# The row of maxima of the second and fourth attention goes through DRAM by DMA in a four-layer cross-attention kernel

## The chip, the cores and the metric

The kernel runs on one core of one Trainium2 chip, as one launch. The metric is the device time of that launch in microseconds. Lower is better.

## The reference, cut to what matters

The model has four layers on 2048 tokens (8 sequences of 256) of width 128. Each layer is a cross attention onto a context of 256 tokens of width 96 per sequence and then a feed-forward part; both are scaled by a tanh gate and added to the residual `x`. The change touches the second and the fourth attention (`L1` and `L3`), which have the same form with other weights:

```
x = x + jnp.tanh(g_xattn[1]) * _L1_xattn_ref(_layernorm(x, axis=-1), ctx_768, Wq, Wk, Wv, Wo, bo)

def _L1_xattn_ref(x, context, Wq, Wk, Wv, Wo, bo):
    q = (x @ Wq).reshape(B, Nq, 16, 64)
    k = (context @ Wk).reshape(B, Nk, 16, 64)
    v = (context @ Wv).reshape(B, Nk, 16, 64)
    scores = jnp.einsum('bqhd,bkhd->bhqk', q, k) / sqrt(64)
    attn = jax.nn.softmax(scores, axis=-1)
    out = jnp.einsum('bhqk,bkhd->bqhd', attn, v).reshape(B, Nq, 1024)
    return out @ Wo + bo
```

Each query attends to the 256 context tokens of its own sequence, in 16 heads. The third attention (`L2`) has 8 heads of 128 and lets each query attend to all 2048 context tokens; the first has 16 heads of 8.

## The kernel before, in words

**Folding.** For each head the product of the query and key weights is formed once (`A`, 128x96), and that of the value and output weights too (`C`, 96x129 with a column that gives the denominator). So a head's queries are `A` times the normalised tokens, in the 96 dimensions of the context, and both scores and values use the context itself. Precision comes from splitting each operand in a high and a low float16 part and adding three products.

**The function.** `attention(nc, M, layer)` (L736) does the second, third and fourth attention. The third is `wide`; the other two, narrow, are those that the change is about. The queries are worked through in blocks of 512 (`NQ` = 4 blocks per head, so 64 blocks in 16 heads). The five engines each run their own stream, with semaphores between them, and the order of the work in a block is written out by hand in three lists at L783 to L785, one for TensorE, one for VectorE, one for ScalarE. In block (h, qb) the streams do work for three heads' worth of stages at once:

- "q": the queries of head h+1, block qb (`queries`, three matmuls L874 to L876 into job bank 0); ScalarE copies them to `q_hi` (L997) and VectorE makes `q_lo` (L1057), which frees bank 0.
- "st": the scores of the next block, keys on partitions (`scores`, 12 matmuls of 256 columns, L913 to L915).
- "m" 0 and 1: rough scores with queries on partitions (`maxscores`, two matmuls of 256 columns each, L894, into job bank 2), of which VectorE takes the negated maxima per query into `nmax` (L1067).
- "r": the row of maxima (`maxrow`, L900). The maxima lie as columns, one query per partition. Four matmuls with one stationary column each and the identity as moving operand (L905) turn them to a row of 512 in bank 0, once that is free; ScalarE copies the row to partition 96 of `q_hi` (L1002), which frees bank 0. The matmul of `scores` with a contraction of 97 then subtracts the maximum as part of the product.
- "exp" on ScalarE (L1009, L1011), "lo" on VectorE (L1097), "av" 0 and 1 on TensorE (the values, 12 matmuls of 256 columns, L925 to L927, into one bank), "u" on ScalarE (copies their result out, L1034).
- "o" 0 and 1: the projection of the previous block's result (`project` of TensorE, L938, four matmul passes of 129 columns into job bank 1). VectorE takes the reciprocal of the denominators ("d", L1081) and adds the two tiles to `x` ("x", L1091), which frees bank 1. "o" 0 and "o" 1 both use bank 1, so "o" 1 waits for "x" 0.

TensorE's order in a block is

```
q, st, m 0, av 0, o 0, r, av 1, m 1, o 1
```

and VectorE's is `q, m 0, d 0, x 0, lo, m 1, d 1, x 1`; ScalarE's is `q, exp, r, u`. The maxima taken in a block are those of the block four further on; the row made in a block is that of the block three further on (`row_of`, `maxrow(blk + NQ - 1, ...)`), and the scores computed in a block are those of the next one.

**The prologue of an attention** does "q", "m 0", "m 1" and "r" for the four blocks of head 0 (no "r" after the last of them), one after the other, since "q" and "r" share bank 0. Then come the first scores. **The last head** prepares no next head: its blocks have no "q" and no "m", and only its first has an "r".

SyncE issues no DMA and GpSimd does nothing but set semaphores while an attention of this function runs.

Of the kernel before, what the change touches and what calls it, by code (L numbers as in the profile page):

```python
# [79 lines left out]
def persistent(nc, ctx):  # L80
    M = Memory()

    def sb(name, shape, dt):
        return ctx.enter_context(nc.sbuf_tensor(name, shape, dt))

    M.x = sb("x_res", [P, NT, D], F32)
    M.xn = sb("x_norm", [P, NT, D], F32)
    M.xt = sb("x_normT", [P, NTOK], F32)
    M.xt_hi = sb("x_normT_hi", [P, NTOK], F16)
    M.xt_lo = sb("x_normT_lo", [P, NTOK], F16)  # L90
    M.ct_hi = sb("ctxT_hi", [DA, NTOK], F16)
    M.ct_lo = sb("ctxT_lo", [DC, NTOK], F16)
    M.cv_hi = sb("ctx_hi", [P, NT, P], F16)
    M.cv_lo = sb("ctx_lo", [P, NT, P], F16)
    M.A_hi = [n and sb(f"A{n}_hi", [P, L.H, DC], F16) for n, L in enumerate(LAYERS)]
    M.A_lo = [n and sb(f"A{n}_lo", [P, L.H, DC], F16) for n, L in enumerate(LAYERS)]

    M.C = [n and sb(f"C{n}", [DA, L.H + 1, L.CW + 1], F32) for n, L in enumerate(LAYERS)]
    M.w0q_hi, M.w0q_lo = sb("w0q_hi", [P, QB], F16), sb("w0q_lo", [P, QB], F16)
    M.w0k_hi, M.w0k_lo = sb("w0k_hi", [DA, QB], F16), sb("w0k_lo", [DA, QB], F16)  # L100
    M.w0v_hi, M.w0v_lo = sb("w0v_hi", [DA, QB], F16), sb("w0v_lo", [DA, QB], F16)
    M.b0q = sb("b0q", [P, 4], F32)
    M.mask_q, M.mask_k = sb("mask_q", [P, 8], F32), sb("mask_k", [P, 8], F32)
    M.low = sb("low_rows", [P, 2], F32)
    M.diag_q = sb("diag_q", [P, P], F16)
    M.wo0 = sb("wo0", [P, D], F32)

    M.o_dram = nc.dram_tensor("o_scratch", [16, NTOK, 8], F32, kind="Internal").ap()
    M.obias = sb("out_bias", [P, 4, D], F32)
    M.gate = sb("gates", [P, 8], F32)  # L110
    M.ident = sb("ident", [P, P], F32)
    M.ident16 = sb("ident16", [P, P], F16)
    M.neghalf = sb("neg_half", [P, NT], F32)
    M.one = sb("one", [P, 1], F32)
    M.U = sb("u_out", [DA, 2, QB], F32)
    M.wgq = sb("w_gate_q", [P, INTER], BF16)
    M.wuq = sb("w_up_q", [P, INTER], BF16)
    M.wgs = sb("w_gate_s", [P, 3], F32)
    M.wus = sb("w_up_s", [P, 3], F32)
    M.wdT = sb("w_downT", [P, 3, D], F32)  # L120
    M.clip = sb("clips", [P, 2], F32)
    M.comb = sb("comb", [P, NT, 18], F32)
    M.ps = ctx.enter_context(nc.psum_tensor("ps", [P, 8, 512], F32))
    M.splits = 0
    M.sem_ln = {k: nc.alloc_semaphore(f"ln_{k}") for k in
                ("stat", "var", "rstd", "norm", "transposed", "hi")}
    return M
# [608 lines left out]
def attention(nc, M, layer):  # L736
# [29 lines left out]
    if wide:  # L766
        first_m = (0, 0, 2, 4, 7, 10, 13, 15)
        m = [[("m", k) for k in range(first_m[u], (*first_m, MJ)[u + 1])] for u in range(UQ)]
        tensor_ops = [[("st", 0), *m[u][:-2], ("av", 0), *m[u][-2:-1], ("av", 1), *m[u][-1:]] for u in range(UQ)]
        tensor_ops[0].insert(0, ("q", 0))  # L770
        tensor_ops[1][1:1] = [("r", 0), ("o", 0)]
        tensor_ops[2].insert(3, ("o", 1))
        in_order = [[op for op in ops if op[0] == "m"] for ops in tensor_ops]
        vector_ops = [[*ops[:-1], ("lo", 0), *ops[-1:]] for ops in in_order]
        vector_ops[0].insert(0, ("q", 0))
        vector_ops[1][:0] = [("d", 0), ("x", 0)]
        vector_ops[2][1:1] = [("d", 1), ("x", 1)]
        scalar_ops = [[("exp", 0)] for u in range(UQ)]
        scalar_ops[0].insert(0, ("q", 0))
        scalar_ops[1].append(("r", 0))  # L780
        scalar_ops[UQ - 1].append(("u", 0))
    else:
        tensor_ops = [[("q", 0), ("st", 0), ("m", 0), ("av", 0), ("o", 0), ("r", 0), ("av", 1), ("m", 1), ("o", 1)]]  # L783
        vector_ops = [[("q", 0), ("m", 0), ("d", 0), ("x", 0), ("lo", 0), ("m", 1), ("d", 1), ("x", 1)]]
        scalar_ops = [[("q", 0), ("exp", 0), ("r", 0), ("u", 0)]]  # L785

    def unit_ops(ops, qb, u, prep, last):

# [18 lines left out]
    def job(h, qb, kind, k=0, prep=True):  # L807

        b = bank_of(kind, k)
        blk = qb if h is None else h * NQ + qb  # L810
        if b == 0:
            if h is None:
                return 0, 2 * blk + (kind == "r")
# [13 lines left out]
    with ExitStack() as ctx:  # L827
# [11 lines left out]
        p = [sb(f"p{i}", [P, 2 * QB], F32) for i in range(2)]  # L839
        p_hi = [sb(f"p_hi{i}", [P, 2 * QB], F16) for i in range(2)]  # L840
        p_lo = [sb(f"p_lo{i}", [P, 2 * QB], F16) for i in range(2)]
        nmax = sb("neg_max", [P, 2, TQ], F16)
        mpart = sb("max_part", [P, 16], F32)
        rden = sb("rden", [P, TQ], F32)

# [8 lines left out]
        qhi_done = sem("q_hi_done")  # L854
        nmax_done = sem("nmax_done")
        rden_done = sem("rden_done")

        def each_head(eng, head):

# [4 lines left out]
            head(H - 1, 1, False, True)  # L864

        with nc.Block() as block:
            @block.tensor
            def _(pe):
                def queries(h, buf, qb, at):
# [9 lines left out]
                def maxscores(buf, qb, k, at, blk):  # L879
# [11 lines left out]
                    else:  # L891
                        k0 = (2 * qb + k) * SEQ
                        for t in range(2):
                            ins = nc.tensor.matmul(ps[:, bank, t * SEQ:(t + 1) * SEQ],  # L894
                                                   q_hi[buf][0:DC, k0 + t * P:k0 + (t + 1) * P],
                                                   M.ct_hi[0:DC, k0:k0 + SEQ], start=True, stop=True)
                    ins.then_inc(job_ready[b], 1)

# [7 lines left out]
                                               M.ident16[:], start=True, stop=True)  # L906
                    ins.then_inc(job_ready[b], 1)

                def scores(buf, par, qb, u):
                    for c, q0, nq, at, _, _ in pieces(qb, u):  # L910
                        o = ps[:, ST[par] + at // QB, at % QB:at % QB + nq]
                        ks = slice(c * P, (c + 1) * P)
# [30 lines left out]
                def head(h, hh, prep, last):  # L943
                    for qb in range(NQ):
                        blk = h * NQ + qb
                        for u in range(UQ):
                            n = blk * UQ + u
                            par = (qb * UQ + u) % 2
                            for kind, k in unit_ops(tensor_ops, qb, u, prep, last):
# [9 lines left out]
                                elif kind == "st":  # L959
# [1 line left out]
                                    pe.wait_ge(exp_done, 2 * n + 2)  # L961


                                    if last and (qb, u) == (NQ - 2, UQ - 1):
                                        pe.wait_ge(job_free[0], job(h, 0, "r", 0, False)[1] + 2)
                                    nu = (u + 1) % UQ
                                    nq = (qb + (nu == 0)) % NQ
                                    scores(1 - hh if nu == 0 and nq == 0 else hh, 1 - par, nq, nu)
                                elif kind == "av":
                                    if k == 0:  # L970
                                        pe.wait_ge(plo_done, n + 1)
# [4 lines left out]
                for qb in range(NQ):  # L976
                    queries(0, 0, qb, job(None, qb, "q"))
                    for k in range(MJ):
                        maxscores(0, qb, k, job(None, qb, "m", k), qb)
                    if qb < NQ - 1:  # L980
                        maxrow(qb, qb % 2, job(None, qb, "r"))
                pe.wait_ge(job_free[0], job(None, NQ - 2, "r")[1] + 2)
                pe.wait_ge(job_free[0], job(None, NQ - 1, "q")[1] + 2)
                scores(0, 0, 0, 0)
                each_head(pe, head)
                for half in range(2):
                    project(H * NQ, 1, H, half, job(H - 1, NQ, "o", half, False))
# [2 lines left out]
            def _(act):  # L990
# [45 lines left out]

                for qb in range(NQ):
                    queries(0, 0, qb, job(None, qb, "q"))
                    if qb < NQ - 1:
                        maxrow(0, qb, job(None, qb, "r"))  # L1040
                exps(0, 0)
                each_head(act, head)
# [10 lines left out]
            def _(dve):  # L1053
# [46 lines left out]
                def head(h, hh, prep, last):  # L1100
                    for qb in range(NQ):
                        blk = h * NQ + qb
                        for u in range(UQ):
                            n = blk * UQ + u
                            par = (qb * UQ + u) % 2
                            for kind, k in unit_ops(vector_ops, qb, u, prep, last):
                                if kind == "q":
                                    queries(h + 1, 1 - hh, qb, (h + 1) * NQ + qb)
                                elif kind == "m":
                                    maxscores((h + 1) * NQ + qb, qb % 2, k, job(h, qb, "m", k))  # L1110
                                elif kind == "d":
                                    denominators(k, job(h, qb, "o", k, prep))
                                elif kind == "x":
# [4 lines left out]
                for qb in range(NQ):  # L1118
                    queries(0, 0, qb, qb)
                    for k in range(MJ):  # L1120
                        maxscores(qb, qb % 2, k, job(None, qb, "m", k))
                lows(0, 0)
                each_head(dve, head)
                for half in range(2):
# [688 lines left out]
```

## Time and profile before

| what | value |
|---|---|
| time, median of 3 runs | 2751.98 us (2751.69 to 2752.57) |
| time of the profiled execution | 2746.5 us |
| its span, first to last instruction | 2744.6 us |
| mean granted TensorE clock | 0.922 of 2.4 GHz |
| busy, share of the span | TensorE 87%, VectorE 73%, ScalarE 55%, GpSimd 6% |
| DMA, mean over the span | 10 GB/s |

The numbers are averages over stages with different limits. The second attention lies from 377 to 727 us of the span and the fourth from 2242 to 2593 us, so the two take about a quarter of it; what the change is worth is to be read inside them. In the rows below "PEld" is TensorE's load of the stationary operand and "PE" its matmul; matmul ends are modelled, so successive starts tell more than durations.

### The profile page before, as it was taken

The page shows a single profiled execution, that of the slowest core. Times are in us where ns is not written, and L with a number is a line of the kernel's source. Part 1 is how long each engine was busy: PE and PEld are TensorE (multiplying, and loading weights), DVE is VectorE, ACT ScalarE, POOL GpSimd, SP SyncE. Part 2 cuts the span into 40 slices and gives each one's busy share as a digit, 9 for nine tenths or more (in the row PEclk, how much of TensorE's full clock was granted, in tenths as well). Part 3 has the DMA queues.
Part 4 walks back from the last instruction along what each step waited for, and adds up shares of the span by engine and source line. Part 5 has one row for each costly group of instructions (what it writes and reads, how often), then busy time and mean ns, then how long its engine had stood idle before and what let it go on. Part 6 is the DMA issues. An engine that isn't in the chain of part 4 may idle for free. (4 is left out here: it accounts for less than half of the span.)

```text
span 2744.6 us, 47864 instructions
## 1 busy us (share of the span) xinstructions
PE 2376.1 (87%) x16584; PEld 1443.5 (53%) x16585; DVE 2006.3 (73%) x3978; ACT 1505.0 (55%) x2022; POOL 170.8 (6%) x162
## 2 busy tenths in 40 slices
PE   3698359999789986999999999999769969999777
PEld 3343148888556651444444444444346638888644
DVE  2675648888668876787778788885447758888778
ACT  1266227777455541566566666666548836777511
POOL 2100010000022211000000000000012210000000
PEclk9689569999899995999999999999979979999889
DMA  5001000000010000000000000000010000000000
GB/s 137 0 7 12 15 1 1 0 0 0 1 59 23 11 1 0 1 1 1 1 1 1 1 1 1 1 1 1 0 32 24 8 1 1 0 0 0 1 17 25
DMA packets 58145, 26.70 MB, mean 10 GB/s; under 512 B 38443, under 2 KB 54003, under 8 KB 57654
## 3 DMA queue, kind: packets, MB, share of 16 engines
q1 hardware_dynamic: 53396, 22.15, 3.3%
q10 hardware_dynamic: 4610, 2.71, 0.4%
q8 instruction: 86, 1.41, 0.2%
q14 instruction: 53, 0.43, 0.1%
HBM read 22.75 MB, written 2.10 MB: 9 GB/s over the span
## 5 line engine op out<-in xcount | busy, mean ns | idle before, releaser
L1009 ACT ACTIVATE at_p<-ps 128x1024 f32<-128x1024 f32 x384 | 393.3, 1024 | 435.5 <-PE ps L915 435.4
L1097 DVE TENSOR_TENSOR at_p_lo<-at_p,at_p_hi 128x1024 f16<-128x1024 f32 x384 | 468.6, 1220 | 146.1 <-ACT at_p_hi L1011 145.8
L1011 ACT ACTIVATE at_p_hi<-ps 128x1024 f16<-128x1024 f32 x384 | 390.6, 1017 | 0.0
L1064 DVE TENSOR_REDUCE at_max_part<-ps 128x1 f32<-128x512 f32 x512 | 341.3, 687 | 49.1 <-PE ps L889 44.6
L925 PE MATMUL ps<-at_p_hi,ctx_hi 128*128 128x256 f16 (+1 forms) x1024 | 336.1, 328 | 12.4 <-DVE at_p_lo L1097 9.5
L913 PE MATMUL ps<-at_q_hi,ctxT_hi 97*128 97x256 f16 (+1 forms) x1024 | 337.1, 329 | 0.0
L914 PE MATMUL ps<-at_q_hi,ctxT_lo 96*128 96x256 f16 (+1 forms) x1024 | 336.4, 329 | 0.0
L915 PE MATMUL ps<-at_q_lo,ctxT_hi 96*128 96x256 f16 (+1 forms) x1024 | 333.9, 326 | 0.0
L927 PE MATMUL ps<-at_p_lo,ctx_hi 128*128 128x256 f16 (+1 forms) x1024 | 332.9, 325 | 0.0
L926 PE MATMUL ps<-at_p_hi,ctx_lo 128*128 128x256 f16 (+1 forms) x1024 | 332.6, 325 | 0.0
L1700 DVE TENSOR_TENSOR ex_hidden_lo<-ex_hidden,ex_hidden_hi 128x512 f16<-128x512 f32 x256 | 195.4, 766 | 64.1 <-ACT ex_hidden L1657 63.8
L889 PE MATMUL ps<-ctxT_hi,at_q_hi 96*128 96x512 f16 x512 | 208.3, 409 | 20.5 <-DVE x_res L1091 11.5
L938 PE MATMUL ps<-C,u_out 97*128 (+1 forms) x1304 | 203.9, 278 | 6.8 <-DVE x_res L1091 6.0
L1091 DVE SCALAR_TENSOR_TENSOR x_res<-ps,at_rden,x_res 128x128 f32<-128x128 f32 x652 | 198.8, 347 | 11.7 <-DVE at_rden L1081 0.2
L1582 PE MATMUL ps<-x_normT_hi,ex_w_hi 128*128 128x512 f16 x456 | 175.7, 385 | 34.7 <-POOL ex_w_lo L1547 34.5
L1646 ACT ACTIVATE ex_silu<-ps 128x512 f32<-128x512 f32 x164 | 97.9, 597 | 191.3 <-PE ps L1586 189.1
L1613 PE MATMUL ps<-ex_w_hi,ex_hidden_hi 128*128 128x128 f16 x1024 | 176.3, 220 | 20.3 <-DVE ex_hidden_lo L1700 16.7
L938 PEld LDWEIGHTS ps<-C,u_out 97*128 97x128 f32 x1304 | 173.7, 191 | 22.5 <-DVE x_res L1091 9.3
L1067 DVE TENSOR_REDUCE at_neg_max<-ps 128x2 f16<-128x512 f32 x256 | 174.3, 681 | 6.1 <-PE ps L894 5.6
L1709 DVE SCALAR_TENSOR_TENSOR x_res<-ps,comb,x_res 128x128 f32<-128x128 f32 x544 | 152.5, 343 | 35.3 <-PE ps L1617 30.0
L1617 PE MATMUL ps<-ex_w_hi,ex_hidden_lo 128*128 128x128 f16 x1024 | 176.3, 220 | 0.0
L1615 PE MATMUL ps<-ex_w_lo,ex_hidden_hi 128*128 128x128 f16 x1024 | 176.3, 220 | 0.0
(252 smaller groups left out, 4015.1 us busy)
## 6 DMA issues: line engine op xcount, KB each, us to landing
ex_w_raw<-in_L_w SPq DMA_DIRECT2D x8, 512.0 KB, 3.2
ex_w<-in_L_w SPq DMA_DIRECT2D x16, 256.0 KB, 2.8
ex_w_raw<-in_L_w SPq DMA_DIRECT2D x8, 256.0 KB, 2.6
raw<-in_L_q SPq DMA_DIRECT2D x3, 512.0 KB, 10.4
raw<-in_L_o SPq DMA_DIRECT2D x3, 512.0 KB, 12.3
raw<-in_L_k SPq DMA_DIRECT2D x3, 384.0 KB, 7.6
raw<-in_L_v SPq DMA_DIRECT2D x3, 384.0 KB, 9.5
ex_w_raw<-in_L_w SPq DMA_DIRECT2D x9, 128.0 KB
```

The source lines that it names most:

```text
L889: ins = nc.tensor.matmul(ps[:, bank, :], q_hi[buf][0:DC, q0:q0 + P], M.ct_hi[0:DC, kb * QB:(kb + 1) * QB], start=True, stop=True)
L913: nc.tensor.matmul(o, M.ct_hi[:, ks], q_hi[buf][:, q0:q0 + nq], start=True, stop=False)
L914: nc.tensor.matmul(o, M.ct_lo[:, ks], q_hi[buf][0:DC, q0:q0 + nq], start=False, stop=False)
L915: ins = nc.tensor.matmul(o, M.ct_hi[0:DC, ks], q_lo[buf][:, q0:q0 + nq], start=False, stop=True)
L925: nc.tensor.matmul(o, M.cv_hi[:, c, :], p_hi[par][:, cols], start=first, stop=False)
L926: nc.tensor.matmul(o, M.cv_lo[:, c, :], p_hi[par][:, cols], start=False, stop=False)
L927: ins = nc.tensor.matmul(o, M.cv_hi[:, c, :], p_lo[par][:, cols], start=False, stop=last)
L938: ins = nc.tensor.matmul(ps[:, BANKS[b], t * (CW + 1):(t + 1) * (CW + 1)], M.U[:, upar, (2 * half + t) * P:(2 * half + t + 1) * P], C[:, s ...
L1009: nc.scalar.activation(p[par][:].rearrange("p (b q) -> p b q", b=2), s, ACT.Exp, scale=1.0 / QS).then_inc(exp_done, 1)
L1011: nc.scalar.activation(p_hi[par][:].rearrange("p (b q) -> p b q", b=2), s, ACT.Exp, scale=1.0 / QS).then_inc(exp_done, 1)
L1064: nc.vector.tensor_reduce(mpart[:, k:k + 1], ps[:, BANKS[b], :], AX.X, ALU.max).then_inc(job_free[b], 1)
L1097: nc.vector.tensor_tensor(p_lo[par][:], p[par][:], p_hi[par][:], ALU.subtract).then_inc(plo_done, 1)
```

## The change

In the narrow attentions "r" is gone from all three lists, and with it the four matmuls, the ScalarE copy and the two uses of bank 0 per row. SyncE gets a stream of its own: for each row it waits for the maxima, writes them to a DRAM scratch row, waits until they have landed there, and issues a DMA from DRAM to partition 96 of `q_hi`. TensorE waits for that row ahead of each `scores`. `nmax` grows from 2 to 8 slots. The maxima's stationary operand takes every second query, so that each partition holds pairs of neighbouring queries. The third attention keeps its old code (`wide`).

```diff
+    M.row_dram = nc.dram_tensor("row_scratch", [2 * NQ, QB], F16, kind="Internal").ap()
...
-        tensor_ops = [[("q", 0), ("st", 0), ("m", 0), ("av", 0), ("o", 0), ("r", 0), ("av", 1), ("m", 1), ("o", 1)]]
+        tensor_ops = [[("q", 0), ("st", 0), ("m", 0), ("av", 0), ("o", 0), ("av", 1), ("m", 1), ("o", 1)]]
...
-        scalar_ops = [[("q", 0), ("exp", 0), ("r", 0), ("u", 0)]]
+        scalar_ops = [[("q", 0), ("exp", 0), ("u", 0)]]
...
+        if b == 0 and not wide:
+            return 0, qb if h is None else NQ + blk
...
-        nmax = sb("neg_max", [P, 2, TQ], F16)
+        nmax = sb("neg_max", [P, 2 if wide else 2 * NQ, TQ], F16)
...
+            @block.sync
+            def _(sp):
+                if wide:
+                    return
+
+                def row(h, buf, qb):
+                    sp.wait_ge(nmax_done, h * NQ + qb + 1)
+                    sp.dma_start(M.row_dram[buf * NQ + qb, :].rearrange("(k p t) -> p k t", k=2, t=2),
+                                 nmax[:, buf * NQ + qb, :].rearrange("p (k t) -> p k t", k=2)
+                                 ).then_inc(row_spilled[qb], 16)
+                    sp.wait_ge(row_spilled[qb], h * 16 + 16)
+                    sp.dma_start(q_hi[buf][DC:DA, qb * QB:(qb + 1) * QB], M.row_dram[buf * NQ + qb:buf * NQ + qb + 1, :]
+                                 ).then_inc(row_landed[qb], 16)
+
+                def head(h, hh, prep, last):
+                    if prep:
+                        for qb in range(NQ):
+                            row(h + 1, 1 - hh, qb)
+
+                for qb in range(NQ):
+                    row(0, 0, qb)
+                each_head(sp, head)
...
-                                                   q_hi[buf][0:DC, k0 + t * P:k0 + (t + 1) * P],
+                                                   q_hi[buf][0:DC, k0 + t:k0 + SEQ:2],
...
-                def scores(buf, par, qb, u):
+                def scores(buf, par, qb, u, h):
+                    if not wide:
+                        pe.wait_ge(row_landed[qb], h * 16 + 16)
...
-                    if qb < NQ - 1:
+                    if wide and qb < NQ - 1:
                         maxrow(qb, qb % 2, job(None, qb, "r"))
-                pe.wait_ge(job_free[0], job(None, NQ - 2, "r")[1] + 2)
+                if wide:
+                    pe.wait_ge(job_free[0], job(None, NQ - 2, "r")[1] + 2)
```

## Rows read from the trace of the kernel before

**Rows 1.** Windows: busy us (instructions) of each engine, TensorE's granted clock, DMA.

```profile
470.00:695.00 225.00, 225.00 (x1922) 185.89 (x1919) 199.76 (x447) 165.41 (x223) 0.00 (x0) 1.00 0.00 0
2280.00:2560.00 280.00, 280.00 (x2387) 231.14 (x2386) 249.05 (x557) 205.48 (x278) 0.00 (x0) 1.00 0.00 0
```

**Rows 2.** Timeline, one block of the second attention: start, duration, engine, line.

```profile
550.17 0.38 PE L874 MATMUL ps<-x_normT_hi,A_hi 128*96 128x512 f16 x1
...
552.92 0.53 PEld L938 LDWEIGHTS ps<-C,u_out 97*128 97x128 f32 x4
...
553.57 0.20 PEld L905 LDWEIGHTS ps<-ident,at_neg_max 128*1 128x1 f16 x4
...
553.67 0.17 DVE L1081 RECIPROCAL at_rden<-ps 128x2 f32<-128x2 f32 x1 [0.26 <-PE ps L938]
553.88 0.10 PEld L925 LDWEIGHTS ps<-at_p_hi,ctx_hi 128*128 128x128 f16 x1
553.88 0.61 DVE L1091 SCALAR_TENSOR_TENSOR x_res<-ps,at_rden,x_res 128x128 f32<-128x128 f32 x2
...
554.32 0.58 ACT L1002 ACTIVATE at_q_hi<-ps 1x512 f16<-1x512 f32 x1
...
554.66 0.52 PEld L938 LDWEIGHTS ps<-C,u_out 97*128 97x128 f32 x4
...
555.22 0.38 PE L874 MATMUL ps<-x_normT_hi,A_hi 128*96 128x512 f16 x1
...
557.96 0.53 PEld L938 LDWEIGHTS ps<-C,u_out 97*128 97x128 f32 x4
```

**Rows 3.** Waits, 400 to 700 us: engine, tile, line, releaser: us, times, longest.

```profile
DVE at_rden L1081 <- PE ps L938: 15.8, 59, 0.3
```

**Rows 4.** Timeline of the last head, where nothing stands between the projections' halves but values.

```profile
712.60 0.53 PEld L938 LDWEIGHTS ps<-C,u_out 97*128 97x128 f32 x4
...
713.35 0.17 DVE L1081 RECIPROCAL at_rden<-ps 128x2 f32<-128x2 f32 x1 [1.37 <-PE ps L938]
...
713.56 0.61 DVE L1091 SCALAR_TENSOR_TENSOR x_res<-ps,at_rden,x_res 128x128 f32<-128x128 f32 x2
...
714.22 0.52 PEld L938 LDWEIGHTS ps<-C,u_out 97*128 97x128 f32 x4 [0.53 <-DVE x_res L1091]
```

**Rows 5.** Timeline, the prologue of the second attention.

```profile
376.87 0.66 PE L874 MATMUL ps<-x_normT_hi,A_hi 128*96 128x512 f16 x1 [4.52 <-POOLq L1050]
...
379.04 0.69 DVE L1057 TENSOR_TENSOR at_q_lo<-ps,at_q_hi 96x512 f16<-96x512 f32 x1 [4.84 <-ACT at_q_hi L997]
...
380.53 0.61 PE L894 MATMUL ps<-ctxT_hi,at_q_hi 96*128 96x256 f16 x2 [0.79 <-DVE at_neg_max L1067]
...
383.24 0.66 PE L874 MATMUL ps<-x_normT_hi,A_hi 128*96 128x512 f16 x1 [0.68 <-ACT at_q_hi L1002]
...
399.63 0.61 PE L894 MATMUL ps<-ctxT_hi,at_q_hi 96*128 96x256 f16 x2 [0.78 <-DVE at_neg_max L1067]
...
400.03 0.42 PE L913 MATMUL ps<-at_q_hi,ctxT_hi 97*128 97x256 f16 x1
```

**Rows 6.** DMA issues on SyncE of short pieces (ns min/median/max), landing, and a small load.

```profile
L513 SPq DMA_DIRECT2D o_scratch<-at_o x64: 355/507/1664, 161.3 to 270.2; - x64
...
DMA to landing us min/median/max: 1.7/1.9/3.4
...
rt_bias<-in_L_router_b SPq DMA_DIRECT2D x2, 4.0 KB, 1.7
```

**Rows 7.** Instructions by line, 400 to 700 us: count, busy us, mean ns, idle before.

```profile
L938 PEld LDWEIGHTS ps<-C,u_out 97*128 97x128 f32 x468 | 61.3, 191 | 1.5
...
L894 PEld LDWEIGHTS ps<-ctxT_hi,at_q_hi 96*128 96x128 f16 x234 | 22.7, 97 | 2.9
```

**Rows 8.** Windows: second attention's prologue, its first block, the third attention's prologue.

```profile
376.50:383.00 6.50, 3.30 (x11) 1.01 (x11) 2.07 (x3) 0.99 (x2) 0.00 (x0) 0.50 0.00 1
404.00:406.00 2.00, 1.92 (x15) 1.33 (x13) 1.20 (x2) 1.51 (x3) 0.00 (x0) 0.86 0.00 0
1070.00:1080.00 10.00, 6.94 (x16) 1.59 (x16) 6.12 (x11) 1.18 (x2) 0.00 (x0) 0.50 0.00 0
```

More of the change, by code:

```diff
@@ L856, in attention @@
         rden_done = sem("rden_done")
+        row_landed = [sem(f"max_row_landed{qb}") for qb in range(NQ)]
+        row_spilled = [sem(f"max_row_spilled{qb}") for qb in range(NQ)]
         def each_head(eng, head):
@@ L961, in head @@
                                     pe.wait_ge(exp_done, 2 * n + 2)
-                                    if last and (qb, u) == (NQ - 2, UQ - 1):
+                                    if wide and last and (qb, u) == (NQ - 2, UQ - 1):
                                         pe.wait_ge(job_free[0], job(h, 0, "r", 0, False)[1] + 2)
@@ L967, in head @@
                                     nq = (qb + (nu == 0)) % NQ
-                                    scores(1 - hh if nu == 0 and nq == 0 else hh, 1 - par, nq, nu)
+                                    ahead = nu == 0 and nq == 0
+                                    scores(1 - hh if ahead else hh, 1 - par, nq, nu, h + 1 if ahead else h)
                                 elif kind == "av":
@@ L979, in _ @@
                         maxscores(0, qb, k, job(None, qb, "m", k), qb)
-                    if qb < NQ - 1:
+                    if wide and qb < NQ - 1:
                         maxrow(qb, qb % 2, job(None, qb, "r"))
-                pe.wait_ge(job_free[0], job(None, NQ - 2, "r")[1] + 2)
+                if wide:
+                    pe.wait_ge(job_free[0], job(None, NQ - 2, "r")[1] + 2)
                 pe.wait_ge(job_free[0], job(None, NQ - 1, "q")[1] + 2)
-                scores(0, 0, 0, 0)
+                scores(0, 0, 0, 0, 0)
                 each_head(pe, head)
@@ L1038, in _ @@
                     queries(0, 0, qb, job(None, qb, "q"))
-                    if qb < NQ - 1:
+                    if wide and qb < NQ - 1:
                         maxrow(0, qb, job(None, qb, "r"))
@@ L1109, in head @@
                                 elif kind == "m":
-                                    maxscores((h + 1) * NQ + qb, qb % 2, k, job(h, qb, "m", k))
+                                    maxscores((h + 1) * NQ + qb, qb % 2 if wide else (1 - hh) * NQ + qb, k, job(h, qb, "m", k))
                                 elif kind == "d":
@@ L1120, in _ @@
                     for k in range(MJ):
-                        maxscores(qb, qb % 2, k, job(None, qb, "m", k))
+                        maxscores(qb, qb % 2 if wide else qb, k, job(None, qb, "m", k))
                 lows(0, 0)
```

## The prediction

> **What bounds the kernel now.** I read the page for the shares, then the windows of the two attentions that the diff touches, then the timeline of one block, then the waits. The windows [rows 1] show TensorE busy in 225.00 of 225.00 us and in 280.00 of 280.00 us, at the full granted clock (level 2.4 GHz), with 8.54 and 8.53 matmuls per us (count over time): both attentions run in one steady state, and one block may speak for all. VectorE is busy 89% there, ScalarE 74%. In the timeline the block repeats every 555.22 - 550.17 = 5.05 us [rows 2], and TensorE's successive starts leave no hole. VectorE is nearly full too: it loses 0.26 us per block waiting for the first half of the projection, 15.8 us in 59 waits [rows 2, 3]. So TensorE is the bound and VectorE stands close behind it. What a shorter TensorE stream brings depends on what is late next.
>
> **Part 1, the transposing matmuls go.** From the load of the first one-column operand (553.57) to the load of the values' operand behind it (553.88) they hold TensorE 0.31 us per block [rows 2]. With nothing else in the way the block would fall to 5.05 - 0.31 = 4.74 us. VectorE would allow it nearly: without its 0.26 us wait it could repeat in 5.05 - 0.26 = 4.79 us.
>
> But there is a ring through both engines. "o" 0 and "o" 1 share bank 1, so between them lie the reciprocal and the two additions of VectorE. From the load of "o" 0 to that of "o" 1 the steady block takes 554.66 - 552.92 = 1.74 us, and the additions end at 553.88 + 0.61 = 554.49: TensorE comes 0.17 us after its permission, and doesn't wait. Take 0.31 us out between the two and it comes at 1.43 us, ahead of it. How fast the ring can turn, the last head shows: there TensorE did wait for the additions, and load to load took 714.22 - 712.60 = 1.62 us, made of 0.75 to the reciprocal, 0.21 to the additions, 0.61 for them and 0.05 to the load [rows 4]. The same steps stand in the steady block (0.75, 0.21, 0.61 [rows 2]). So the piece shrinks from 1.74 to 1.62, not to 1.43. The rest, from "o" 1 to the next "o" 0, is 557.96 - 554.66 = 3.30 us of unbroken TensorE work that the change leaves alone. New block: 3.30 + 1.62 = **4.92 us**, over the 4.79 of VectorE and the 4.74 of TensorE. Gain 0.12 us per block, while 0.19 us become a new stall of TensorE on the additions.
>
> How many blocks: 15 heads x 4 = 60 in each attention. Of the last head only the first block has an "r", and it is near the ring's time already: nothing. Two attentions: 120 x 0.12 = **14.4 us**. Its bounds: 0.02 us of reading error per block is 2.4 us.
>
> **Part 2, the prologue.** The four rounds of "q, m, m, r" are a chain of latencies at half clock (0.50, level 1.2 GHz [rows 8]). A round with "r" takes 383.24 - 376.87 = 6.37 us; the next "q" waits until ScalarE has copied the row out of bank 0. After the change it waits for `q_lo`, done at 379.04 + 0.69 = 379.73, so it follows the second maxima's matmuls directly. These start at 380.53, and what follows them comes 400.03 - 399.63 = 0.40 later: 380.93 [rows 5]. The round becomes 4.06 us, 2.31 less; the last round has no "r" now. 3 rounds x 2.31 x 2 attentions = **13.9 us**. I take the fourth attention's as the second's: same code, same start from a stalled TensorE.
>
> **Part 3, ScalarE's copy goes**: 0.58 us per block [rows 2], counted at nothing. ScalarE has idle time in every block; the exponentials begin when the scores are there, which TensorE's order sets. The cover is that idle time; it only grows.
>
> **Part 4, the two DMAs per row.** No attention of this function issues one today, so I bound them. The store is 256 pieces of 4 bytes. Nearest is the first attention's store of 512 pieces of 32 bytes: 0.51 us of SyncE to issue, 1.9 us to land, at worst 1.66 and 3.4; a small load lands after 1.7 [rows 6]. SyncE waits for the store, so one row takes it 0.51 + 1.9 + 0.51 = 2.9 us, at the worst issues and landing of the rows 1.66 + 3.4 + 1.66 = 6.7. I take 2.9, since one row comes every 4.92 us and nothing else is on this queue; behind SyncE's wait stand only its own later rows. Delay of a row: 2.9 + 1.7 = 4.6 us. Its cover: the maxima of a block are done before the next block's "o" 0 (557.96), and the scores that need them come after the "q" that starts three blocks after the first (550.17 + 3 x 4.92 = 564.9): at least 6.9 us. In the prologue, row 0 has until 376.87 + 4 x 4.06 = 393.1, with maxima by about 382 (380.53 + 0.61 and one VectorE operation). So it costs nothing; if the cover is gone, TensorE stands ahead of its scores and everything with it. No gain lies here either.
>
> The Trainium skill's page "DMA: Bandwidth & Descriptors" speaks against this route: its "Specifications" say that pieces under 512 bytes are read, modified and written, and "Anatomy of one DMA" puts a fixed cost of about 2 us on each, heaviest when the target is HBM. By that fixed cost the two would take about 4 us, an estimate from that page, and the sum would stay as it is. The trace agrees, with 1.9 us to landing for pieces of 32 bytes [rows 6]; no run here shows 4-byte ones.
>
> **Part 5, the strided operand.** `maxscores` now loads every second float16. The load takes 97 ns today; the float32 operand of the projection, whose elements also lie 4 bytes apart, takes 191 ns, and four of them pass in 0.53 us [rows 2, 7]. Bounds: nothing, or 0.09 us for each of four loads. Loads run beside the matmul ahead, so I take nothing. The Trainium skill, "SBUF — State Buffer", on SBUF's 16-byte lines (under the port map), says a read keeps full rate with at least two hits per line, which this step has; no run shows it yet.
>
> **Part 6**: the DRAM row, the larger `nmax` and SyncE's part in the stage's end are small and beside other work: nothing.
>
> **Sum.** 14.4 + 13.9 = 28.3 us. Against the profiled execution's 2746.5 us (span 2744.6) that is 2718.2. The runs' median is 2751.98, 5.5 above that execution; I take the same difference off it: **2723.7 us**. A measurement of this kernel can tell about 0.2%, 5.5 us, from no change.
>
> **The rivals.**
>
> *Slower: SyncE cannot keep up.* Place: the wait for the store between the two DMAs, once per row. For it speak 4-byte pieces, shorter than any in the trace, and single issues of 1.66 us; against it the median of 2.9 us per row. If a row took longer than 4.92 us of SyncE, the block would take that. The gain is eaten from 5.05 + 13.9/120 = 5.17 us per row on, slower than can be missed from 5.21; at 6.7 us per row it is (6.7 - 5.05) x 120 - 13.9 = +184, 2936 us. Chance 0.04.
>
> *The strided load is dear.* With 0.09 us more per load, the two of "m" 1 fill the new 0.19 us stall and cost nothing, the two of "m" 0 lie in the 3.30 us: 0.18 x 120 = 21.6 us, leaving 28.3 - 21.6 = 6.7, so 2745. It needs loads that no longer hide behind 256 columns; the four float32 loads in 0.53 us speak against. Chance 0.08, half of it within 0.2%.
>
> *The clock rises in the prologue.* It is denser after the change. PE busy time of a round is 3.30 us at 0.50; halved, it would give at most 1.65 x 4 = 6.6 us, and the half clock that reaches into the first block until about 404.4 (clock 0.86 in 404 to 406) would give half of 4.4, 2.2: 8.8 per attention, 17.6 more, 2706 us. Against it stands the third attention's prologue, with TensorE busy 6.94 of 10 us and still at 0.50 [rows 8]. The Trainium skill's "TensorE: Matmul & The Clock Gate", Part 1, says that activity releases the throttle; the rise after the first scores agrees. Chance 0.06.
>
> *The ring isn't there,* and all of 0.31 us is gained or most of it: 120 x 0.31 + 13.9 = 51 us, 2701. [Rows 4] speak against it directly. Chance 0.02.
>
> **How the numbers follow.** My forecast has 0.80. The clock's later steps may fall some us earlier or later when all is shifted, the reading of the ring is good to 2.4 us, and the runs to about 3; its own range is 2715 to 2733. The range reaches on towards the dearer load and the earlier clock: 2711 to 2738. Faster by over 0.2%: 0.80 + 0.06 + 0.02 + half of 0.08 = 0.92, less 0.01 for what I don't see: 0.91; within 0.2%: 0.04 + 0.01 = 0.05; slower 0.04.
>
> **What would show it.** In the changed trace: a period of 4.92 us; a wait of TensorE for the additions ahead of "o" 1, once per block, its load 1.62 us after that of "o" 0; VectorE's wait for the first projection still there, at about 0.13 us; prologue rounds of 4.06 us at clock 0.50; SyncE about 2.9 us per row and idle between; no wait of TensorE for a DMA. I am wrong if TensorE waits for a row, if the loads of the maxima's operand grow from 97 ns and their matmuls lie further apart, or if the period is 4.8 or less.

## The result, and the profile after

The changed kernel takes 3162.67 us (median of 4 runs, 3160.67 to 3163.65) against 2752.25 us (4 runs, 2751.69 to 2752.57) for the kernel before, measured together: a ratio of 1.149, 95% interval 1.147 to 1.151. It is **410 us slower**, where 28 us faster was forecast. The time lies far outside the range of 2711 to 2738. Of the runs of the kernel before that stood beside the first experiments, one took 8331.95 us; it is in no ratio below.

The profiled execution of the changed kernel took 3160.67 us, with a span of 3158.9 us. The windows of the second attention come first, with the columns of [rows 1] (PE, PEld, DVE, ACT, POOL, granted clock, DMA share, GB/s):

```profile
470.00:695.00 225.00, 164.73 (x1049) 123.67 (x1048) 123.30 (x270) 84.44 (x108) 0.00 (x0) 0.84 0.02 0
```

TensorE ran 1049 matmuls in a stretch that held 1922 before, and was idle for 60 of 225 us. Its granted clock fell from 1.00 to 0.84, a mixture of both levels. Two neighbouring windows show them:

```profile
567.30:577.30 10.00, 6.58 (x50) 4.85 (x48) 7.69 (x17) 4.32 (x6) 0.00 (x0) 1.00 0.03 0
577.50:580.70 3.20, 3.20 (x16) 2.21 (x15) 0.14 (x1) 0.57 (x1) 0.00 (x0) 0.50 0.00 0
```

In the first, at 2.4 GHz, TensorE stood for 3.4 of 10 us; in the second it works without a pause at 1.2 GHz. What it waits for stands in the page's costliest groups (line numbers have moved: L943 is the first matmul of "st", L1099 the maxima's operation):

```profile
L943 PE MATMUL ps<-at_q_hi,ctxT_hi 97*128 97x256 f16 (+1 forms) x1024 | 361.1, 353 | 284.9 <-DMA at_q_hi<-row_scratch 284.6
...
L1099 DVE TENSOR_REDUCE at_neg_max<-ps 128x2 f16<-128x512 f32 x256 | 176.0, 687 | 320.4 <-PE ps L922 319.8
...
row_scratch<-at_neg_max SPq DMA_DIRECT2D x128, 1.0 KB, 7.9
at_q_hi<-row_scratch SPq DMA_DIRECT2D x128, 1.0 KB
```

The last two lines are the new DMAs. The store, 1.0 KB per row, takes **7.9 us** from issue to landing. For [rows 6], the nearest row of before, that was 1.9 us. SyncE's waits (us in total, times, longest), and the scratch tile's own view with the issues:

```profile
SPq L883 <- DMA row_scratch<-at_neg_max: 969.8, 128, 9.2
```

```profile
L879 SPq DMA_DIRECT2D row_scratch<-at_neg_max x128: 359/360/380, 384.1 to 2981.6; - x128
L883 SPq DMA_DIRECT2D at_q_hi<-row_scratch x128: 241/242/263, 391.9 to 2990.1; - x128
...
DMA to landing us min/median/max: 7.3/7.9/9.6
```

SyncE spends 970 us waiting for 128 stores, 7.6 us each. Issuing is cheap, 0.36 and 0.24 us. The timeline shows how this becomes the block's period (the first and the last row here are the second attention's first and last store):

```profile
384.06 0.37 SPq L879 DMA_DIRECT2D row_scratch<-at_neg_max  x1
...
582.36 0.24 SPq L883 DMA_DIRECT2D at_q_hi<-row_scratch  x1
...
582.74 0.36 SPq L879 DMA_DIRECT2D row_scratch<-at_neg_max  x1
...
585.49 0.27 PE L943 MATMUL ps<-at_q_hi,ctxT_hi 97*128 97x256 f16 x1 [1.39 <-DMA at_q_hi<-row_scratch]
...
590.55 0.24 SPq L883 DMA_DIRECT2D at_q_hi<-row_scratch  x1
...
590.91 0.36 SPq L879 DMA_DIRECT2D row_scratch<-at_neg_max  x1
...
910.67 0.36 SPq L879 DMA_DIRECT2D row_scratch<-at_neg_max  x1
```

From store to store SyncE turns in 590.91 - 582.74 = 8.17 us: 7.81 until the store has landed and the load is issued, 0.36 to the next store. The mean over the 63 turns of this attention is (910.67 - 384.06) / 63 = 8.36 us. In 121 of the 128 rows SyncE doesn't wait for the next row's maxima, so nothing pauses in between, and a block can't be shorter than one row. TensorE starts 3.1 us after the load was issued (582.36 to 585.49). The load itself is quick: by the semaphore events in the trace it lands 2.6 us after its issue (median of 128 rows), and in less than 3.5 us in 125 of them.

In the three others it takes 6.5, 6.7 and 8.2 us. The longest of these is in the block where TensorE's matmuls wait longest in this attention:

```profile
599.17 0.24 SPq L883 DMA_DIRECT2D at_q_hi<-row_scratch  x1
...
599.52 0.36 SPq L879 DMA_DIRECT2D row_scratch<-at_neg_max  x1
...
607.37 0.40 PE L943 MATMUL ps<-at_q_hi,ctxT_hi 97*128 97x256 f16 x1 [7.43 <-DMA at_q_hi<-row_scratch]
```

The DMA view counts the packets that moved in two stretches of this block, first 599.3 to 601.6 us, then 601.6 to 607.3:

```profile
DMA packets 274, 0.00 MB, mean 1 GB/s; under 512 B 273, under 2 KB 274, under 8 KB 274
```

```profile
DMA packets 0, 0.00 MB, mean 0 GB/s; under 512 B 0, under 2 KB 0, under 8 KB 0
```

Between 599.3 and 601.6 us all packets of the store and the load have passed; between 601.6 and 607.3 there isn't one. The block at 582.74 is no different: its packets have passed by 585.5, and the store lands at 590.5. By these records the last 5 to 6 us are no transfer time: the bytes are under way in 2 us, and the completion comes late.

### The profile page after: what moved, and what is told of

It reads as the page before. It is cut to its first block and busy times, and to the rows that moved or that the text cites. A ratio compares the mean times of both kernels' runs of the same rounds, so it can differ in the third digit from the quotient of the medians.

```text
span 3158.9 us, 46906 instructions
## 1 busy us (share of the span) xinstructions
PE 2511.8 (80%) x16072; PEld 1496.1 (47%) x16073; DVE 2017.1 (64%) x3978; ACT 1429.9 (45%) x1894; POOL 170.6 (5%) x162
## 5 line engine op out<-in xcount | busy, mean ns | idle before, releaser
L943 PE MATMUL ps<-at_q_hi,ctxT_hi 97*128 97x256 f16 (+1 forms) x1024 | 361.1, 353 | 284.9 <-DMA at_q_hi<-row_scratch 284.6
L1099 DVE TENSOR_REDUCE at_neg_max<-ps 128x2 f16<-128x512 f32 x256 | 176.0, 687 | 320.4 <-PE ps L922 319.8
L955 PE MATMUL ps<-at_p_hi,ctx_hi 128*128 128x256 f16 (+1 forms) x1024 | 362.7, 354 | 11.8 <-DVE at_p_lo L1129 8.9
L944 PE MATMUL ps<-at_q_hi,ctxT_lo 96*128 96x256 f16 (+1 forms) x1024 | 363.7, 355 | 0.0
L945 PE MATMUL ps<-at_q_lo,ctxT_hi 96*128 96x256 f16 (+1 forms) x1024 | 363.3, 355 | 0.0
L956 PE MATMUL ps<-at_p_hi,ctx_lo 128*128 128x256 f16 (+1 forms) x1024 | 358.2, 350 | 0.0
L957 PE MATMUL ps<-at_p_lo,ctx_hi 128*128 128x256 f16 (+1 forms) x1024 | 356.3, 348 | 0.0
L943 PEld LDWEIGHTS ps<-at_q_hi,ctxT_hi 97*128 97x128 f16 x1024 | 106.6, 104 | 408.4 <-issue 212.6
L968 PE MATMUL ps<-C,u_out 97*128 (+1 forms) x1304 | 237.2, 309 | 9.1 <-DVE x_res L1123 5.8
L968 PEld LDWEIGHTS ps<-C,u_out 97*128 97x128 f32 x1304 | 198.6, 215 | 52.0 <-DVE x_res L1123 36.0
L1113 DVE RECIPROCAL at_rden<-ps 128x2 f32<-128x2 f32 x326 | 55.2, 169 | 194.5 <-PE ps L968 167.6
```

The source lines that it names most:

```text
L943: nc.tensor.matmul(o, M.ct_hi[:, ks], q_hi[buf][:, q0:q0 + nq], start=True, stop=False)
L944: nc.tensor.matmul(o, M.ct_lo[:, ks], q_hi[buf][0:DC, q0:q0 + nq], start=False, stop=False)
L945: ins = nc.tensor.matmul(o, M.ct_hi[0:DC, ks], q_lo[buf][:, q0:q0 + nq], start=False, stop=True)
L955: nc.tensor.matmul(o, M.cv_hi[:, c, :], p_hi[par][:, cols], start=first, stop=False)
L956: nc.tensor.matmul(o, M.cv_lo[:, c, :], p_hi[par][:, cols], start=False, stop=False)
L957: ins = nc.tensor.matmul(o, M.cv_hi[:, c, :], p_lo[par][:, cols], start=False, stop=last)
```

## The experiments

**Is it the store, and would the rest of the forecast have held?** The first four kernels share their runs of before (median 2753.17 us). The theory by then: neighbouring 4-byte pieces in DRAM make the store slow, and all else in the forecast holds. The rivals: any store of 4-byte pieces is slow, the route by DMA is slow in itself, or a removed part wasn't worth what I thought.

*Padded.* Each 4-byte piece gets 64 bytes of DRAM of its own; number, size and source of the pieces stay.

```diff
-    M.row_dram = nc.dram_tensor("row_scratch", [2 * NQ, QB], F16, ...)
+    M.row_dram = nc.dram_tensor("row_scratch", [2 * NQ, QB // 2, 32], F16, ...)
...
-   sp.dma_start(M.row_dram[buf * NQ + qb, :].rearrange("(k p t) -> p k t", k=2, t=2), ...
+   sp.dma_start(M.row_dram[buf * NQ + qb, :, 0:2].rearrange("(k p) t -> p k t", k=2), ...
```

> Each 4-byte piece of the row gets a stretch of 64 bytes of its own in DRAM; number and size of pieces, queue and waits stay. In the changed kernel all 4-byte packets of a row are moved within about 1.1 us of their start, yet the store's completion comes 7.9 us after its issue. Theory A (the acknowledgement waits because 16 neighbouring pieces are written into the same 64 bytes one after the other): the store lands in 2 to 3 us, SyncE takes under 4.9 us per row, and the kernel comes near 2724 to 2760 us (the load now gathers 256 pieces and may be later). Theory B (a store of 256 pieces of 4 bytes to DRAM is this slow wherever they go): landing stays near 8 us and the time near 3160 us or above.

Measured: 2719.41 us, one run; once more with five rounds, 2726.09 us (2720.50 to 2731.61), ratio 0.990 [0.989, 0.992]. Expected of the repeat:

> The row with each 4-byte piece in 64 bytes of its own, timed now in rounds: 2717 to 2727 us, 28 us under the kernel before as the forecast had it.

The page's rows of the same two DMAs, in the first of these kernels:

```profile
row_scratch<-at_neg_max SPq DMA_DIRECT2D x128, 1.0 KB, 1.6
...
at_q_hi<-row_scratch SPq DMA_DIRECT2D x128, 1.0 KB, 2.5
```

The same 256 pieces of 4 bytes land in 1.6 us instead of 7.9, and the load in 2.5 although it now gathers 256 pieces. A store is reported complete in 16 parts: in the changed kernel the first comes 5.1 us after the issue and the last 7.9 us (medians from the semaphore events), in the padded one all come between 1.4 and 1.6. One edit of addresses brings 3162.67 - 2726.09 = 437 us, and the change is then faster than before. Size and number of the pieces are not the cause; their being neighbours in DRAM is.

*Direct.* No DRAM: two DMAs per row go from `nmax` straight to partition 96, where their pieces are neighbours too.

```diff
+   for k in range(2):
+       sp.dma_start(q_hi[buf][DC:DA, qb * QB + k * SEQ:qb * QB + (k + 1) * SEQ],
+                    nmax[:, buf * NQ + qb, 2 * k:2 * k + 2]).then_inc(row_landed[qb], 16)
```

> No DRAM: two DMAs per row go straight from the columns of maxima to partition 96 of the query buffer, 128 pieces of 4 bytes each, and SyncE waits for no DMA. Computes the reference. Theory A and B: the slow step is the write to DRAM, so each lands in about 2 us, nothing waits for a row, and the block takes the 4.92 us of the forecast: 2715 to 2733 us. Theory C (many 4-byte pieces are slow to be acknowledged at any target): landing of 6 us or more; even then SyncE does not wait between rows, and with 7 us of cover the time would stay under 2800 us.

```profile
at_q_hi<-at_neg_max SPq DMA_DIRECT2D x256, 0.5 KB, 2.0
```

Measured: 2725.7 us (4 runs, 2720.98 to 2729.23), ratio 0.990 [0.987, 0.992]; 128 neighbouring pieces of 4 bytes land in SBUF in 2.0 us. Neighbours are harmless there.

*No row.* The DMAs go altogether; partition 96 is set to zero once, so no maximum is subtracted. Everything else of the change stays. It measures parts 1, 2, 3 and 5 of the forecast alone.

```diff
-                    sp.dma_start(M.row_dram[buf * NQ + qb, :] ...
...
-                        pe.wait_ge(row_landed[qb], h * 16 + 16)
+                        pe.wait_ge(row_landed[0], 2)
```

> No row is written at all: partition 96 of the query buffer is set to zero once, TensorE waits for that alone, SyncE has no stream. The maxima are computed and not subtracted. This leaves parts 1, 2, 3 and 5 of the forecast without the DMAs. Forecast: 2718 us beside a profiled execution of 2746.5, 28 us under the kernel before, with a block of 4.92 us and prologue rounds of 4.06 us. Rival (the ring over the projection's bank does not bind): block 4.75 to 4.80 us, 42 to 50 us under. Rival (the strided operand costs): block over 5.0 us.

Measured: 2721.37 us (4 runs, 2719.00 to 2722.08), ratio 0.988 [0.986, 0.990]; the profiled execution took 2722.08 us. Its timeline of a block, the counterpart of [rows 2]:

```profile
550.07 0.12 PEld L879 LDWEIGHTS ps<-x_normT_hi,A_hi 128*96 x1
...
552.86 0.68 DVE L1079 TENSOR_REDUCE at_neg_max<-ps 128x2 f16<-128x512 f32 x1
552.92 0.53 PEld L945 LDWEIGHTS ps<-C,u_out 97*128 97x128 f32 x4
...
553.67 0.17 DVE L1093 RECIPROCAL at_rden<-ps 128x2 f32<-128x2 f32 x1
...
553.88 0.61 DVE L1103 SCALAR_TENSOR_TENSOR x_res<-ps,at_rden,x_res 128x128 f32<-128x128 f32 x2
...
554.54 0.52 PEld L945 LDWEIGHTS ps<-C,u_out 97*128 97x128 f32 x4 [0.31 <-DVE x_res L1103]
...
554.99 0.12 PEld L879 LDWEIGHTS ps<-x_normT_hi,A_hi 128*96 x1
```

The block takes 554.99 - 550.07 = 4.92 us; load to load of the projection 554.54 - 552.92 = 1.62; the second load now waits for VectorE's additions. The prologue's four "q":

```profile
382.26 0.66 PE L879 MATMUL ps<-x_normT_hi,A_hi 128*96 128x512 f16 x1 [4.59 <-POOLq L1062]
...
386.32 0.63 PE L879 MATMUL ps<-x_normT_hi,A_hi 128*96 128x512 f16 x1
...
390.35 0.63 PE L879 MATMUL ps<-x_normT_hi,A_hi 128*96 128x512 f16 x1
...
394.38 0.63 PE L879 MATMUL ps<-x_normT_hi,A_hi 128*96 128x512 f16 x1
```

Rounds of 4.06, 4.03 and 4.03 us, against 6.37 in [rows 5].

The last addition of the second attention, in the kernel before and in this one, gives the whole stage:

```profile
726.38 0.61 DVE L1091 SCALAR_TENSOR_TENSOR x_res<-ps,at_rden,x_res 128x128 f32<-128x128 f32 x2
```

```profile
717.76 0.61 DVE L1103 SCALAR_TENSOR_TENSOR x_res<-ps,at_rden,x_res 128x128 f32<-128x128 f32 x2
```

From the first "q" to the end of this addition it takes 726.99 - 376.87 = 350.1 us before and 718.37 - 382.26 = 336.1 without rows. In the fourth attention it is 350.3 and 336.4 by the same rows. The two gains, 14.0 and 13.9 us, are free of what happens outside the attentions. That matters, because the second attention starts at 377 us in some executions and at 382 to 385 in others.

*Stride.* The kernel before, with the strided operand alone.

```diff
-                                                   q_hi[buf][0:DC, k0 + t * P:k0 + (t + 1) * P],
+                                                   q_hi[buf][0:DC, k0 + t:k0 + SEQ:2],
```

> The kernel before with one edit: the stationary operand of the rough scores takes every second query. The maxima go to the wrong neighbours, the work is the same. Forecast: load of that operand stays at 97 ns and the time within 0.1% of the kernel before. Rival: the load takes some 190 ns and the time rises by 10 to 40 us.

```profile
L894 PEld LDWEIGHTS ps<-ctxT_hi,at_q_hi 96*128 96x128 f16 x174 | 17.0, 98 | 2.1
```

Measured: 2746.47 us, one run, 0.03 us from the profiled execution of before. The load takes 98 ns against the 97 of [rows 7], and the two attentions take 350.2 and 350.4 us against 350.1 and 350.3. The stride costs nothing that can be seen.

**How close is too close?** Padded kernels with a piece every 32, 16 and 8 bytes (a width of 16, 8 and 4 in the diff, which is against the padded kernel; before, beside them: 2757.41 us). By then I had two points, 1.6 us for a piece alone and 7.9 for eight per 32 bytes, and drew a line between them.

```diff
-    M.row_dram = nc.dram_tensor("row_scratch", [2 * NQ, QB // 2, 32], F16, ...)
+    M.row_dram = nc.dram_tensor("row_scratch", [2 * NQ, QB // 2, 16], F16, ...)
```

> The padded row with one 4-byte piece per 32 bytes, so 2 per 64 bytes. One per 64 bytes landed in 1.6 us, 16 per 64 bytes (the changed kernel) in 7.9. Theory A with a cost per neighbour: 6.3 us over 15 neighbours is 0.42 each. If the unit that neighbours share is 64 bytes: 1.6 + 0.4 = 2.0 us. If it is 32 bytes: 1.6 us. Time as with 64 bytes, 2719 us within 0.3%.

> One 4-byte piece per 16 bytes, 4 per 64. Unit of 64 bytes: 1.6 + 3 x 0.42 = 2.9 us to landing. Unit of 32 bytes, where the dense row has 8 per unit at 0.9 us each: 2.5 us. Rival (only truly adjacent pieces hurt, a threshold): 1.6 us. Time again near 2720.

> One 4-byte piece per 8 bytes, 8 per 64. Unit of 64 bytes: 1.6 + 7 x 0.42 = 4.5 us to landing; SyncE then needs some 5.2 us per row or more and the time begins to rise, to 2730 to 2790 us. Unit of 32 bytes: 4.3 us. Rival threshold: 1.6 us and no rise.

The store's row of the page at 16 and at 8 bytes, one kernel each:

```profile
row_scratch<-at_neg_max SPq DMA_DIRECT2D x128, 1.0 KB, 2.0
```

```profile
row_scratch<-at_neg_max SPq DMA_DIRECT2D x128, 1.0 KB, 3.0
```

At 32 bytes it is 1.6 us, as at 64. The times are 2723.07, 2719.42 and 2724.64 us, one run each, all within the spread of the padded kernel. One, two, four and eight pieces per 32 bytes give 1.6, 2.0, 3.0 and 7.9 us. At 32 bytes that is the value of a unit of 32 bytes; the estimate with a unit of 64 had 2.0. At 16 and 8 bytes both linear estimates were too high (2.5 or 2.9 for 2.0, 4.3 or 4.5 for 3.0): the growth is slow first and steep at the end.

**Pieces, or pieces per 32 bytes?** The dense row once with 128 pieces of 8 bytes (which sends maxima to other queries than their own), once as two DMAs of 128 pieces of 4 bytes, one after the other (before: 2756.72 us).

```diff
+   sp.dma_start(M.row_dram[buf * NQ + qb, :].rearrange("(p c) -> p c", p=P), nmax[:, buf * NQ + qb, :]) ...
```

> The changed kernel's dense row of 1 KB, written as 128 pieces of 8 bytes, one per partition, in place of 256 pieces of 4. Changes which maximum goes to which query; the work is the same. If the acknowledgement depends on how many pieces share 32 bytes (8 in the changed kernel: 7.9 us; 4: 3.0; 2: 2.0; 1: 1.6), it is 3.0 us with 4 per 32 bytes, SyncE is quick enough and the time is near 2722 us. Rival (it is the 1 KB without gaps that is slow, whatever the pieces): 7.9 us and 3160.

```diff
+   for k in range(2):
+       sp.dma_start(M.row_dram[buf * NQ + qb, k * SEQ:(k + 1) * SEQ].rearrange("(p t) -> p t", t=2),
+                    nmax[:, buf * NQ + qb, 2 * k:2 * k + 2]).then_inc(row_spilled[qb], 16)
+       sp.wait_ge(row_spilled[qb], h * 32 + 16 * k + 16)
```

> The dense row written as two DMAs of 128 pieces of 4 bytes, each 512 bytes, the second issued when the first has landed. Pieces per 32 bytes stay at 8, their number per DMA halves. If each group of 32 bytes has its own queue of writes (density alone counts): 7.9 us for each half, SyncE needs 17 us per row and the time rises to some 4100 us. Rival (the number of colliding writes in flight counts): about 4 us or less for each half, some 9 us per row together or less, and 3200 us or below.

The store's rows, first of the eight-byte kernel, then of the one with halves:

```profile
row_scratch<-at_neg_max SPq DMA_DIRECT2D x128, 1.0 KB, 2.9
```

```profile
row_scratch<-at_neg_max SPq DMA_DIRECT2D x256, 0.5 KB, 7.3
```

Eight-byte pieces, four per 32 bytes, take 2.9 us, as the 4-byte ones at the same density (3.0), and half as many of them: 2727.43 us. Half a dense row of 4-byte pieces still takes 7.3 us, so a row costs two such waits: 4025.2 us. Both are one run each. The number of pieces hardly matters, their density does. And against the direct kernel, whose DMAs have the same 128 pieces of 4 bytes at the same density, the destination alone is another: 2.0 us in SBUF, 7.3 in DRAM.

**Can the dense store be hidden?** SyncE issues the next row's store before it loads the row ahead of it.

```diff
+                            store_row(h + 1, 1 - hh, qb)
+                            load_row(*((h + 1, 1 - hh, qb - 1) if qb else (h, hh, NQ - 1)))
```

> The changed kernel's dense row, but SyncE issues the next row's store before it waits for this one's and issues the load. If the 7.9 us are a latency that two stores can share, a row is ready some 4.9 + 3 + 0.7 + 2 = 10 to 11 us after its maxima, 1 to 2 us over the cover of about 9, and the block settles where three periods cover it: 5.0 to 5.6 us, 2730 to 2810 us. If it is a throughput (the writes queue up one behind the other in memory), two stores take twice as long and the time stays near 3160 us.

Measured: 2916.93 us, one run, between the two values expected. It hit neither. One row in its timeline, from the store's issue to the scores that it releases (other rows' DMAs lie between):

```profile
590.72 0.36 SPq L879 DMA_DIRECT2D row_scratch<-at_neg_max  x1
...
598.91 0.24 SPq L885 DMA_DIRECT2D at_q_hi<-row_scratch  x1
...
604.36 0.28 PE L950 MATMUL ps<-at_q_hi,ctxT_hi 97*128 97x256 f16 x1 [1.85 <-DMA at_q_hi<-row_scratch]
```

The row needs 604.36 - 590.72 = 13.6 us: 8.2 for the store and 5.4 from the issue of a load that runs behind the next store. The store is no slower than in the changed kernel (8.0 us to landing at the median, against 7.9), although the next one is issued before it lands: two stores in flight don't lengthen each other here. The load is slower: 4.3 us at the median of the 128 rows, against 2.6 in the changed kernel, where it is issued ahead of the store. Now SyncE is no longer the bound; the delay of a row is, since its cover is only between two and three blocks. The period becomes 6.4 us (597.44 less 590.72 is 6.7 for one of them; the mean comes from 207 operations on the denominators in 220 us, six per block). What I hadn't priced was the slow load, with 2 us in the expectation.

**Can the stall of the ring be used?** The padded kernel with "o" 0 moved ahead of "av" 0, so that both value products lie between the halves of the projection.

```diff
-        tensor_ops = [[("q", 0), ("st", 0), ("m", 0), ("av", 0), ("o", 0), ("av", 1), ("m", 1), ("o", 1)]]
+        tensor_ops = [[("q", 0), ("st", 0), ("m", 0), ("o", 0), ("av", 0), ("av", 1), ("m", 1), ("o", 1)]]
```

> The padded row, and TensorE's order is q, st, m 0, o 0, av 0, av 1, m 1, o 1: the first half of the projection comes ahead of all values, so 12 matmuls of values (1.3 us) lie between the two halves instead of 6 and TensorE does not come back to bank 1 before the additions are done. If the ring is what holds the block at 4.92 us, it falls to TensorE's own 4.74 or VectorE's 4.71 to 4.79, and the kernel takes (4.92 - 4.77) x 120 = 18 us less than the padded one: about 2702 us. Rival (something else holds it): no gain.

Waits from 470 to 690 us; the padded kernel's row first, then three of this one:

```profile
PEld ps L968 <- DVE x_res L1123: 14.0, 45, 0.3
```

```profile
PEld ps L968 <- issue: 7.0, 21, 0.4
DVE at_p_lo L1129 <- ACT at_p_hi L1043: 3.7, 21, 0.2
PEld ps L968 <- DVE x_res L1123: 2.4, 7, 0.4
```

Measured: 2712.05 us (5 runs, 2709.16 to 2716.01), ratio 0.985 [0.984, 0.986]; it beats both kernels. The stall on the additions falls from 45 waits to 7 (14.0 to 2.4 us); 21 waits ahead of the same loads, 7.0 us, have no releaser in the profile and may be part of it. The period is 4.84 us (273 operations in 220 us), not 4.77: in about every other block VectorE now waits for ScalarE's exponential. Against the padded kernel the gain is 14.0 us between the medians, where 18 was expected. The period gives (4.92 - 4.84) x 120 = 9.6 us, and the two attentions are 5.9 and 4.5 us shorter than in the repeated padded kernel (330.2 and 331.6 us against 336.1 and 336.1), 10.4 together; the rest lies outside them.

## Why the prediction was wrong

**Parts 1, 3 and 5 were right.** The block fell to 4.92 us, the ring turned in 1.62, TensorE's new wait for the additions is there in each of 45 blocks, and nothing of the gain is left over for ScalarE's copy (no run takes it out alone). VectorE's gap ahead of the reciprocal shrank from 0.26 us to 553.67 - (552.86 + 0.68) = 0.13, as said. The strided load costs nothing.

**Part 2 was right**, with rounds of 4.06, 4.03 and 4.03 us. The rival of the clock didn't come true: the whole prologue stays at 0.50. The rise to 1.00 comes 21 us after the first "q" in both padded executions and in the one without rows (between 398 and 399 us with the start at 377.6, between 403 and 404 with starts at 382.7 and 382.3), and 27 to 28 us after it before. That is the prologue's shortening and no more.

Together: forecast 28.3 us; measured inside the two attentions 14.0 + 13.9 = 27.9. The whole times scatter more: 31.8 between the medians of before and of the kernel without rows, 24.4 between their profiled executions, and 26.6 with both DMAs per row in the padded form (2752.67 - 2726.09). Part of that scatter arises ahead of the second attention: the two padded executions differ by 5.1 us in all, and their attentions start 5.1 us apart.

**Part 4 failed**, in the step "SyncE waits for the store, so one row takes it 0.51 + 1.9 + 0.51 = 2.9 us, at the worst ... 6.7". The issue was rather cheaper than that, 0.36 and 0.24 us. The landing was 7.9 us, four times the row that I took and twice its worst case. The sentence had named that the pieces are 4 and not 32 bytes, and then priced them by the 32-byte row. A 32-byte piece fills 32 bytes by itself; of these, eight share them. The runs show that this is the condition that decides: at one piece per 32 bytes, the forecast's price (1.6 to 1.9 us) holds for 4-byte pieces also.

**The rival's mechanism was right, its chance and its price were not.** "SyncE cannot keep up" named the place and the point from which it decides, 5.21 us per row. With the measured mean of 8.36 its own formula gives (8.36 - 5.05) x 120 - 13.9 = +383 us; measured was +410. The 27 us between them are missing from the formula. SyncE paces 63 blocks of each attention and not 60, the last head's too: from the first addition to `x` to the last it takes 527.4 us in the second attention, against 319.4 before. And the prologue, which waits for SyncE as well, saves 2.1 and 1.8 us up to the first addition, and not 7 in each attention. In all the attentions take 556.0 and 554.9 us, 410.5 more than before: the slowdown lies in them. The end of its range, 6.7, was treated as a bound of an operation that no row showed; it bounds only what the rows showed. A chance of 0.04 stood on that end.

Part 4's price of 1.7 us for the load was too low as well (2.6), but that cost nothing here. The section that the prediction cites for a fixed cost of 2 us, "Anatomy of one DMA" in the Trainium skill's "DMA: Bandwidth & Descriptors", describes DMAs issued by GpSimd. These are SyncE's: a spaced store took 1.6 us, a dense one 7.9.

A load can be late behind such a store. Issued ahead of it, it lands after 2.6 us at the median; issued behind it, in the reordered kernel, after 4.3. The Trainium skill's "DMA: Bandwidth & Descriptors", section "Queues, rings and completion order", says that the write which reports completion lands only after all earlier writes of that DMA engine. By that rule a load behind a slow store reports late and one ahead of it doesn't, and the two medians agree. The three late loads of the changed kernel were issued ahead of the store too, and the order of issue doesn't explain them. Their reports come within 16 ns of one of the store's 16, where in the 125 other rows the nearest is at least 1.4 us away. That they stood behind the store on one engine is likely, but not shown. The Trainium skill's "Collectives: The Full Stack", under its rules for kernel authors, asks for buffers of collectives aligned to 32 bytes to avoid a read-modify-write. The 1.6 us at one piece per 32 bytes agree with that unit, but what happens inside the memory wasn't seen.

**Left open:** why the delay grows so steeply from four to eight pieces per 32 bytes, and whether it matters which DMA engines write the neighbours. Neither was tried. It also stays open why some executions reach the second attention at 377 us and others 5 to 8 us later.

## What to carry to other kernels

A store from partitions to DRAM in pieces of a few bytes is to be laid out with one piece per 32 bytes: the spacing alone made 437 us here, and the reader of the row can gather it for 2.5 us. When an engine waits for a store between two DMAs, its landing time is a period and not a delay; compute the landing from which it sets the pace, and if the nearest row differs in kind from the new operation, don't use that row's worst case as an upper bound. When work is taken out of one engine's stream, look for the ring through a shared bank that turns next: here it kept back 0.19 of 0.31 us per block, and moving one item in the order regained 0.08 of them. Read a gain of some us inside the stages that were changed, from their first to their last instruction, since whole executions scatter by as much.

## What the runs showed of the hardware that I had not expected

- Landing of a 1 KB store to DRAM by its density: 1.6 us with 4-byte pieces 64 or 32 bytes apart, 2.0 at 16, 3.0 at 8, 7.9 dense; 2.9 for dense 8-byte pieces; 7.3 for half a dense row of 4-byte pieces.
- The same 4-byte pieces, dense, land in SBUF in 2.0 us.
- The delay comes after the last packet's record: none moved between 601.6 and 607.3 us, while the store's landing took 8.2 us. The 16 parts of a dense store's completion come from 5.1 to 7.9 us after the issue, those of a spaced one from 1.4 to 1.6.
- A 1 KB load issued 0.4 us ahead of such a store lands after 2.6 us at the median, but after 6.5 to 8.2 in 3 of 128 rows; one issued behind it, in the reordered kernel, after 4.3.
- TensorE, idle for 60 of 225 us, was granted 0.84 of its clock over the stretch instead of 1.00, with stretches at 0.50 and at 1.00. The matmuls were slower for it; SyncE set the pace, so that should have cost nothing more, though no run shows it alone.
